# Four-block metaformer kernel on one core: a new order of TensorE's and ScalarE's work in one software-pipelined step

## What is computed

```
x = x + gated attention over the image axis (16 images) at each (a, b); 8 heads of 16
t = t + sum over the top 2 of 8 experts (router softmax) of t_norm @ expert_w + expert_b
x = x + (primary * sigmoid(EMA scan over a of the gating half)) @ W_con.T + b_con
t = t + soft top-8 token picks by 32 experts per image, pooled, MLP with gelu, scattered back
```

## Time and profile before

| what | us |
|---|---|
| median of three runs | 3147.93 (3114.8 to 3160.26) |
| time of the profiled execution | 3123.18 |
| its span | 3121.5 |
| first to last row maxima (L817, x128) | 63.2 to 2796.8 |
| TensorE busy | 2647.5 (85%) |
| VectorE busy | 2551.6 (82%) |
| GpSimd busy | 2161.0 (69%) |
| ScalarE busy | 2005.1 (64%) |
| mean granted TensorE clock | 0.839 of full speed |

### The profile page before, as it was taken

One profiled execution on the slowest core, in us unless ns is written; L12 is line 12 of the kernel. 1 busy time (PEld: TensorE's weight loads), 2 busy tenths in 40 slices (PEclk: granted clock), 3 DMA queues, 4 the chain that ended last, 5 costly groups with the idle time before them and its releaser, 6 DMA issues. The chain is left out here.

```text
span 3121.5 us, 108500 instructions
## 1 busy us (share of the span) xinstructions
PE 2647.5 (85%) x37071; PEld 1969.9 (63%) x37071; DVE 2551.6 (82%) x9002; ACT 2005.1 (64%) x3590; POOL 2161.0 (69%) x2963
## 2 busy tenths in 40 slices
PE   2898898888888888898898898888988988896697
PEld 2666666666666656666666666666666666664586
DVE  2788889888888898888888888888889888885604
ACT  2666767766676676776776766677667676762600
POOL 2677777877777777777787877778777777863000
PEclk9788988887888888888887987889889788885858
DMA  0011101111011010110101111011010010101828
GB/s 17 9 20 18 19 17 19 19 18 19 17 19 18 18 19 17 19 19 18 19 17 18 19 18 19 17 19 19 18 19 18 17 19 18 19 15 19 269 96 337
DMA packets 263153, 106.67 MB, mean 34 GB/s; under 512 B 250257, under 2 KB 254900, under 8 KB 258997
## 3 DMA queue, kind: packets, MB, share of 16 engines
q1 hardware_dynamic: 260933, 93.16, 12.9%
q10 hardware_dynamic: 2160, 12.68, 1.0%
HBM read 55.31 MB, written 50.33 MB: 34 GB/s over the span
## 5 line engine op out<-in xcount | busy, mean ns | idle before, releaser
L472 ACT ACTIVATE kT<-s_bank,b_k,block_of 128x512 f32<-128x512 f32 x1024 | 748.8, 771 | 3.6 <-PE s_bank L609 0.3
L640 PE MATMUL s_bank<-kT,qT 128*32 128x128 f32 x8192 | 396.1, 372 | 187.3 <-issue 187.3
L640 PEld LDWEIGHTS s_bank<-kT,qT 128*32 128x32 f32 x8192 | 349.5, 152 | 226.8 <-issue 224.7
L489 ACT ACTIVATE qT<-shared,b_qkg 128x256 f32<-128x256 f32 x256 | 107.5, 471 | 412.0 <-PE shared L609 412.0
L811 DVE TENSOR_REDUCE mixed<-yg 128x256 f32<-128x2048 f32 x128 | 288.5, 2254 | 0.2
L687 PEld LDWEIGHTS o_bank<-w_o,ogT 128*128 128x128 f32 x2048 | 247.9, 193 | 23.7 <-DVE ogT L839 14.8
L414 POOL TENSOR_TENSOR probs<-weights,own_den 128x1024 f32<-128x1024 f32 x128 | 252.7, 1975 | 1.8 <-DVE own_den L857 1.8
L687 PE MATMUL o_bank<-w_o,ogT 128*128 128x64 f32 x2048 | 246.9, 274 | 4.3 <-DVE ogT L839 3.9
L387 POOL TENSOR_TENSOR split_ffn<-norm_ffn,split_ffn 128x256 fp32r<-128x256 f32 x128 | 93.6, 731 | 215.1 <-ACT split_ffn L464 215.1
L658 PEld LDWEIGHTS o_bank<-probsT,v_sb 32*32 32x32 f32 x16384 | 170.2, 107 | 63.7 <-issue 58.1
L658 PE MATMUL o_bank<-probsT,v_sb 32*32 32x64 f32 x16384 | 196.5, 234 | 1.5 <-DVE yg L932 1.5
(11 more groups left out here) (204 smaller groups left out, 7648.6 us busy)
## 6 DMA issues: line engine op xcount, KB each, us to landing
x_in<-in_x SPq DMA_DIRECT2D x1024, 16.0 KB, 1.7
x_scratch<-x SPq DMA_DIRECT2D x1024, 16.0 KB, 1.4
normalized_x_scratch<-norm_pick SPq DMA_DIRECT2D x1024, 16.0 KB, 1.5
xa<-normalized_x_scratch SPq DMA_DIRECT2D x16, 1024.0 KB, 8.1
xb<-x_scratch ACTq DMA_DIRECT2D x8, 1024.0 KB, 10.3
out_x<-xa SPq DMA_DIRECT2D x16, 512.0 KB, 5.3
out_x<-xb SPq DMA_DIRECT2D x16, 512.0 KB, 6.9
xa<-x_scratch SPq DMA_DIRECT2D x4, 1024.0 KB, 6.5
```

The lines of the kernel that those rows point to most:

```text
L472: ins = s.activation(kT[:, h, :], bk("k")[:], ACT.Identity, bias=b_k[:, h:h + 1], scale=block_of[:, h:h + 1])
L640: ins = t_.matmul(s_bank[g * 32:(g + 1) * 32, 0, t * P:(t + 1) * P], qT[z][:, c, tok:tok + 32], kT[:, :, tok + c * N:tok + (c + 1) * N], s ...
```

## The change

Nothing is computed in another way; only orders, one lag and the bank turns change. The transposes att_t are made in the step of their half (lag 0) near TensorE's step end, and their copy to zT is behind the last masked key in ScalarE. TensorE begins a step with q, then come the scores, k, and the values. conv_t comes ahead of route and pick. The experts come as y0, y1, y3, then att_t, then y2. In ScalarE the first two masked keys come right behind q and the ffn rounding, ahead of exp and the copies of ffn_t and v; the att rounding comes behind the v copy; the conv rounding comes behind two more keys and the gate. VectorE reads y3 ahead of y2.

The new ScalarE step as a list: q copy, ffn rounding, keys 0 and 1, exp, ffn_t copy, v copy, att rounding, keys 2 and 3, gate, conv rounding, keys 4 and 5, pick_t copy, conv_t copy, key 6, pick copy, router's exp, four expand copies, key 7, zT copy, gT plus one, tanh of the scan. The diff below is cut to the lines that move.

```diff
-LAG = {"att_t": 1, "k": 1, "q": 1, "gate": 1, "v": 1, "scores": 2,
+LAG = {"att_t": 0, "k": 1, "q": 1, "gate": 1, "v": 1, "scores": 2,
-TURNS = ["att_t", "q", "ffn_t", "v", "scan_out", "gate", "pick", "conv_t", "y0", "expand", "y3"]
+TURNS = ["q", "ffn_t", "v", "scan_out", "gate", "conv_t", "pick", "expand", "y0", "y3", "att_t"]
 # ScalarE
-                    if runs(i, q, 1):
-                        act.wait_ge(filled["att_t"], at(i, q, 1))
-                        wait(act, filled["k"], at(i, q, 3))
-                        s.copy(zT[z1][:], bk("att_t")[:]).then_inc(drained["att_t"], 1)
-                    if runs(i, q, 4):
-                        round_part("ffn", i, q, 4, "ffn_t")
...
-                    if runs(i, q, 0):
-                        round_part("att", i, q, 0, "att_t")
+                    if runs(i, q, 4):
+                        round_part("ffn", i, q, 4, "ffn_t")
+                    if runs(i, q, 1):
+                        act.wait_ge(filled["k"], at(i, q, 1))
+                        wait(act, s_scores, at(i, q, 2))
+                        masked_keys(range(0, 2))
+                    if runs(i, q, 2):
+                        act.wait_ge(s_sub, at(i, q, 2))
+                        s.activation(weights[:], weights[:], ACT.Exp, scale=float(C) ** -0.5).then_inc(s_exp, 1)
...
+                    if runs(i, q, 0):
+                        round_part("att", i, q, 0, "att_t")
+                    if runs(i, q, 1):
+                        masked_keys(range(2, 4))
...
+                        masked_keys(range(7, H)).then_inc(drained["k"], 1)
+                    if runs(i, q, 0):
+                        act.wait_ge(filled["att_t"], at(i, q, 0))
+                        wait(act, filled["gate"], at(i, q, 2))
+                        s.copy(zT[q][:], bk("att_t")[:]).then_inc(drained["att_t"], 1)
 # TensorE
                     if runs(i, q, 1):
-                        bank_free(pe, i, q, "att_t")
-                        pe.wait_ge(s_split["att"], at(i, q, 1))
-                        transposed("att_t", "att", i, q, 1)
+                        pe.wait_ge(drained["att_t"], at(i, q, 1))
+                        project("q", 0)
...
-                        pe.wait_ge(drained["att_t"], at(i, q, 1))
-                        project("q", 0)
+                        project("k", 1)
...
                         project("gate", 2)
-                        project("k", 1)
...
+                    if runs(i, q, 5):
+                        bank_free(pe, i, q, "conv_t")
+                        pe.wait_ge(s_split["conv"], at(i, q, 5))
+                        transposed("conv_t", "conv", i, q, 5)
                     if runs(i, q, 4):
                         pe.wait_ge(drained["ffn_t"], at(i, q, 4))
...
-                    if runs(i, q, 5):
-                        bank_free(pe, i, q, "conv_t")
-                        pe.wait_ge(s_split["conv"], at(i, q, 5))
-                        transposed("conv_t", "conv", i, q, 5)
-                    if runs(i, q, 4):
-                        experts(0)
...
                     if runs(i, q, 4):
-                        for t in range(1, QT):
-                            experts(t)
+                        experts(0)
+                        experts(1)
+                        experts(3)
+                    if runs(i, q, 0):
+                        bank_free(pe, i, q, "att_t")
+                        pe.wait_ge(s_split["att"], at(i, q, 0))
+                        transposed("att_t", "att", i, q, 0)
+                    if runs(i, q, 4):
+                        experts(2)
 # VectorE
-                        dve.wait_ge(drained["y3"], at(i, q, 5))
+                        dve.wait_ge(drained["y2"], at(i, q, 5))
...
-                        for t in range(2, QT):
+                        for t in (3, 2):
```

More of the change, by code:

```diff
@@ L496, in step @@
                         act.wait_ge(filled["ffn_t"], at(i, q, 4))
-                        wait(act, filled["y3"], at(i, q, 6))
+                        wait(act, filled["y2"], at(i, q, 6))
                         s.copy(tT[z][:], bk("ffn_t")[:]).then_inc(drained["ffn_t"], 1)
@@ L513, in step @@
                                      scale=0.5).then_inc(drained["gate"], 1)
-                        act.wait_ge(filled["k"], at(i, q, 1))
-                        wait(act, s_scores, at(i, q, 2))
-                        masked_keys(range(0, 2))
                     if runs(i, q, 5):
                         round_part("conv", i, q, 5, "conv_t")
+                    if runs(i, q, 1):
+                        masked_keys(range(4, 6))
                     if runs(i, q, 8):
@@ L524, in step @@
                         s.copy(lT[:], bk("pick_t")[0:D, :]).then_inc(drained["pick_t"], 1)
+                    if runs(i, q, 5):
+                        act.wait_ge(filled["conv_t"], at(i, q, 5))
+                        wait(act, filled["expand"], at(i, q, 6))
+                        s.copy(cT[:], bk("conv_t")[:]).then_inc(drained["conv_t"], 1)
                     if runs(i, q, 1):
-                        masked_keys(range(2, 4))
+                        masked_keys(range(6, 7))
                     if runs(i, q, 8):
@@ L532, in step @@
                         s.activation(dst, src, ACT.Identity, bias=gb_col[:]).then_inc(drained["pick"], 1)
-                    if runs(i, q, 5):
-                        act.wait_ge(filled["conv_t"], at(i, q, 5))
-                        wait(act, filled["expand"], at(i, q, 6))
-                        s.copy(cT[:], bk("conv_t")[:]).then_inc(drained["conv_t"], 1)
                     if runs(i, q, 4):
@@ L541, in step @@
                         s.activation(lge[:], lgm[:], ACT.Exp).then_inc(s_ratio, 1)
-                    if runs(i, q, 1):
-                        masked_keys(range(4, 6))
                     if runs(i, q, 5):
@@ L557, in step @@
                     if runs(i, q, 1):
-                        masked_keys(range(6, 7))
+                        masked_keys(range(7, H)).then_inc(drained["k"], 1)
[3 more added lines that the diff above has]
+                        s.copy(zT[q][:], bk("att_t")[:]).then_inc(drained["att_t"], 1)
+                    if runs(i, q, 1):
                         act.wait_ge(drained["gate"], at(i, q, 1))
@@ L564, in step @@
                         s.activation(ema_t[:], ema[:].rearrange("p n a -> p a n"), ACT.Tanh, scale=0.5).then_inc(s_emat, 1)
-                    if runs(i, q, 1):
-                        masked_keys(range(7, H)).then_inc(drained["k"], 1)
                 slots(act, step)
```

4 lines of the change are left out of this document (removed).

## The result

The changed kernel takes 3604.52 us, the median of four runs (3603.43 to 3606.9), against 3134.16 us for the kernel before (four runs, 3114.8 to 3160.26): a ratio of 1.1496 with a 95% interval of 1.1398 to 1.1594. Slower was right. The forecast, 3450 us, is 155 us short, and the measured time lies 70 us above the range. The profiled execution took 3606.9 us, with a span of 3605.2 and a mean granted clock of 0.717 (forecast: near 0.72; before: 0.839). Of one kernel further down (after, both) a run at a lower clock than its three others, 3478.99 us, is left out of the time.

A forecast was written before the change was run, and what follows sets the result against it. It took a ring through TensorE and ScalarE, VectorE close behind, to bound the kernel. A step of 24.4 against 21.66 us, times 120 steps, adds 329 to 3123: rounded to 3450 us, range 3370 to 3535.

The forecast's parts named there:

- the chain: Late att rounding in ScalarE delays GpSimd's second att part to 4.47 and second conv part to 9.8 us, holding conv_t.
- The hole: TensorE idle between pick_t and conv_t, waiting for GpSimd's second conv part: 2.5 us a step.
- the two delays: Att rounding behind v, 1.7 to 2.1 us coming through; conv_t ahead of route and pick, logits not before 11.4.
- the place of the idle time decides the clock: On TensorE, idle time and light work ahead of the experts drop the clock every step until the scores: near 0.72.
- route from 10.4 to 11.4, pick to 11.9: TensorE behind conv_t: route ends at 11.4, pick at 11.9 us behind the row maxima, then expand and experts.
- I take the middle: Clock returning during the scores: a step of 24.4 us, between 23.7 (at the first score) and 25.1.
- The rest: y3 ahead of y2, VectorE's read order and bank turns: nothing at the low clock, up to 1 us at the high.
- My upper end, 25.1: Longest step forecast: 11.9 us to expand plus 13.2 at the low clock, scores to row maxima at 3.50.
- The first: Rival: TensorE's clock falls about as often as now, a step of 21.3 to 22.2, 3080 to 3190 us; chance 0.2.
- the third: Rival: both delays real, but low clock covers the experts in half the steps: about 23.1, 3295 us; chance 0.15.
- The second: Rival: TensorE runs ahead, its hole covered; the step is VectorE's own work, 20.4 us, about 2970 us; chance 0.15.
- the removed ring: TensorE's scores to k and ScalarE's gate to last key; cutting it removes 1.36 us idle ahead of the scores.

The follow-up runs named there:

- after, both: The changed kernel with the att rounding ahead of exp and conv_t behind route and pick: 3410.15 us, interval of the ratio to before 1.0787 to 1.0917.
- experiment 1: Att rounding moved ahead of exp in the changed kernel: 3292.03 us; moved behind the v copy in the kernel before: 3288.41 us.
- experiment 2: conv_t moved behind route and pick in the changed kernel: 3641.81 us; moved ahead of route and pick in the kernel before: 3391.3 us.
- Ten dummies: The changed kernel with ten added 128x512 TensorE products, output not used, behind pick_t and ahead of conv_t: 3309.43 us.
- experiment 4: The changed kernel with two added 128x512 TensorE products, output not used, between q and the scores: 3566.47 us.
- the rebuilt order with four dummies: Changed kernel, att rounding ahead of exp, conv_t behind pick, y0 ahead of expand, pick copy ahead of conv_t copy, four unused products behind pick_t: 3240.31 us.
- the kernel before with four: The kernel before with four added 128x512 TensorE products, output not used, between att_t and the scores: 3092.29 us.

## Why the prediction was right or wrong

**Right: the direction and the chain.** The second att part starts at 1522.38 - 1518.21 = 4.17 us behind the row maxima (forecast 4.47), the second conv part ends at 9.47 (9.8), conv_t starts at 9.62 (9.9). The hole is 2.7 us (2.5). The clock is 0.717 (near 0.72), the experts take 1.68 to 1.69 us each, the wait ahead of the scores is gone. These places are measured from the row maxima, which at the median come 0.3 us later behind the scores' end than in the step of the earlier trace rows; from the scores' end conv_t starts at 10.0 in 65 of 81 steps, as forecast. Of the two delays the rounding's place is shown by doing and undoing it (experiment 1), conv_t's only in the kernel before and with a bank turn in the price (experiment 2).

**Right: the place of the idle time decides the clock, and the clock is the largest part of the price.** Ten dummies return 295 of the 470 us, without moving anything else. The row to remember is TensorE's busy share: 86% after, 85% before, with a clock of 0.717 and 0.839. The Trainium skill ("Perfetto Trace Analysis", Matmul Optimizations) says that the matmul engine's power goes by its utilization and that matmuls should run back to back; the second half agrees with these runs, while the utilization, taken over the run, would have called the two kernels equal.

**Wrong: the time, by the price of conv_t, route and pick.** The forecast of a step was 2.8 from the scores to the row maxima (the middle of 3.50 and about 2.0), 9.9 to conv_t, 2.0 to the start of expand, and 9.72 from there to the next scores (0.99 + 6.76 + 0.98 + 0.99). Measured from starts on TensorE, in the step shown and as means over 81 steps of the stretch:

| part of the step | forecast | step shown | mean | mean less forecast |
|---|---|---|---|---|
| scores to conv_t (1527.83 - 1515.20) | 12.7 | 12.63 | 13.06 | +0.36 |
| conv_t to expand (1530.94 - 1527.83) | 2.0 | 3.11 | 2.94 | +0.94 |
| expand to scores (1540.55 - 1530.94) | 9.72 | 9.61 | 9.60 | -0.12 |
| sum | 24.4 | 25.35 | 25.59 | +1.18 |

- *"route from 10.4 to 11.4, pick to 11.9"* is the step that failed, with 0.94 of the 1.18 us. I let the clock fall "before the experts start" but priced route at the 0.96 us and conv_t at the 0.5 us of the high clock. The hole lies ahead of them, so they run low too: conv_t 1528.71 - 1527.83 = 0.88, route 1530.35 - 1528.71 = 1.64. With ten dummies in the hole the same part takes 1.91 us, the forecast's 2.0: it is the clock. The weight loads of route take longer at the low clock as well, first before, then after (lowest, median and highest ns). VectorE's logits, forecast at 11.4, start at 12.25.

```profile
L700 PEld LDWEIGHTS o_bank<-w_router,tT x776: 190/192/192, 614.7 to 2694.7; 128*128 128x128 f32 x194
```
```profile
L702 PEld LDWEIGHTS o_bank<-w_router,tT x656: 190/333/338, 607.1 to 2681.6; 128*128 128x128 f32 x164
```

- *"I take the middle"*: the clock does return around the scores, and they take 2.86 us at the mean, from 1.95 to 3.64. The middle was a guess between two ends and came out by luck. What it lacked is VectorE's tail, which holds TensorE's next conv_t by 0.9 us more in 16 of 81 steps (experiment 4). The prediction had filed the new places of y2 and y3 under *The rest*, as "it costs nothing"; it costs 0.2 us a step.

25.58 - 21.66 = 3.92 us more a step are 470 us over 120 steps; the two profiled executions lie 484 apart, and 14 us are outside these steps. My upper end, 25.1, took the scores at 3.50, which is more than they take, and was still too low, because it has the same 2.0.

**The rivals.** The first (clock as often as now) and the third (half the steps) fall by the rows of L624: every one of these products runs at the low clock, in every step. The second, VectorE's own work at 20.4 us a step, falls too. No kernel here came near it: in steps with the clock at 1.00 throughout, the rebuilt order with four dummies takes 21.38 us. That is 0.2 us less than the kernel before with four, and all that the removed ring was seen to bring.

## What to carry to other kernels

Price a new hole together with everything behind it at the low clock, small products bound by weight loading included, up to the row where the trace shows the clock return. To find what a step consists of, add up one engine's work and its waits: where they fill the stretch, as TensorE's do here, another engine's long tail is beside the path, and the sum should be made in that engine's starts. An edit in the order moves bank turns and copies too; look at the waits of each test kernel before its time is read as the price of one move. And where the trace shows the clock falling in a place, a few dummy products there are a cheap experiment: they tell the price of the clock from the price of the order, and can stay in if they pay (here 1.4%).

## What was new about the hardware

- TensorE's clock is a price of its own: added work made kernels faster by 295 us (ten dummies), 43 us (four, in the kernel before) and 38 us (two ahead of the scores, in the changed kernel, one run).
- The clock fell behind short waits, and busy TensorE alone didn't bring it back: in the changed kernel TensorE's only long idle time is 2.7 us a step, and behind it the clock is 0.50 while TensorE is busy without a break from 1528.7 to 1542.7 us, expert products of 128x512 included. It returned around the scores.
- Products of 8 columns go from 0.96 us for eight at the high clock to 1.72 at the low one; in the kernel before with conv_t early, a product of the ffn transposes takes 273 ns (median, high clock) and one of the att transposes 421 ns (low).
- VectorE's product of 64 x 256 (L807) takes 423 ns at the median, and up to 1518 ns where GpSimd runs a large product beside it; GpSimd's own 128 x 1024 product goes from 1.93 to 2.12 us there.
